# Reordering the first pass of a four-layer graph network kernel: where the aggregation, its casts and the transfers stand

## What is computed

```python
A_norm = A + eye(n);  deg = A_norm.sum(0) + A_norm.sum(1) - diagonal(A_norm);  dinv = rsqrt(deg)
agg = einsum('nm,bmd->bnd', A_norm * dinv[:, None] * dinv[None, :], x).reshape(-1, 256)
h   = relu(batchnorm(agg @ W1.T + b1))      # W1: 512 x 256, statistics over all 8192 rows
out = batchnorm(h @ W2.T + b2)              # W2: 256 x 512
```

## Time and profile before

| what | us |
|---|---|
| median of three runs (lowest, highest) | 2016.44 (2013.59, 2018.27) |
| time of the profiled execution | 2013.94 |
| its span in the trace | 2012.1 |
| TensorE busy | 1944.8 (97%) |
| TensorE weight loads busy | 1730.6 (86%) |
| VectorE busy | 1718.2 (85%) |
| ScalarE busy | 1443.6 (72%) |
| GpSimd busy | 187.8 (9%) |

### The profile page before, as it was taken

One profiled execution on the slowest core, in us unless ns is written; L12 is line 12 of the kernel. 1 busy time (PEld: TensorE's weight loads), 2 busy tenths in 40 slices (PEclk: granted clock), 3 DMA queues, 4 the chain that ended last, 5 costly groups with the idle time before them and its releaser, 6 DMA issues.

```text
span 2012.1 us, 85711 instructions
## 1 busy us (share of the span) xinstructions
PE 1944.8 (97%) x37031; PEld 1730.6 (86%) x37031; DVE 1718.2 (85%) x4795; ACT 1443.6 (72%) x4475; POOL 187.8 (9%) x258
## 2 busy tenths in 40 slices
PE   6899989999999999999999999999999999999997
PEld 3444469999999999999999999999999999999996
DVE  6779897888888988898889888898889888988866
ACT  5657537777777777767777777777777777777777
POOL 2000010110101010101001110101010101111000
PEclk9999999999999999999999999999999999999999
DMA  7857400000100001000100010000000010000000
GB/s 281 290 196 253 175 2 23 14 13 4 44 3 24 3 3 45 13 13 3 44 14 13 4 44 4 23 3 14 34 13 13 3 45 13 13 3 13 3 3 23
DMA packets 36822, 87.79 MB, mean 44 GB/s; under 512 B 2416, under 2 KB 26992, under 8 KB 32752
## 3 DMA queue, kind: packets, MB, share of 16 engines
q1 hardware_dynamic: 36464, 82.56, 11.8%
HBM read 52.15 MB, written 30.41 MB: 41 GB/s over the span
## 4 chain that ended last, share of the span: by engine, by line
PE 78%; ACT 5%; DVE 4%; issue 1%; POOL 0%; ACTq 0%; DVEq 0%
PE ps L1539 18%; PE ps L1568 11%; PE ps L1548 9%; PE ps L1353 8%; PE ps L1387 7%; PE ps L1575 5%; PE ps L1363 4%; PE ps L1395 3%; PE ps L468 2%; PE ps L1330 2%; ACT pool_mem L1726 2%; PE ps L1320 1%; PE ps L1627 1%; PE ps L1595 1%; PE ps L1441 1%; DVE stats L1849 1%
## 5 line engine op out<-in xcount | busy, mean ns | idle before, releaser
L1726 ACT ACTIVATE pool_mem<-ps,lstm_b 128x64 f32<-128x64 f32 (+2 forms) x2496 | 606.2, 364 | 147.0 <-PE ps L1575 102.6
L1539 PE MATMUL ps<-hl_a,w_hi 128*128 128x64 f16 (+1 forms) x3584 | 361.3, 205 | 1.8 <-DVE hl_a L2005 0.9
L1539 PE MATMUL ps<-hl_a,w_lo 128*128 128x64 f16 (+1 forms) x3584 | 360.8, 205 | 0.0
L1818 POOL TENSOR_TENSOR rstd<-mv,nhalf 128x2 f32<-128x2 f32 x224 | 174.1, 779 | 1592.3 <-DVE mv L1853 1592.3
L1539 PEld LDWEIGHTS ps<-hl_a,w_hi 128*128 128x128 f16 x3584 | 284.4, 97 | 6.3 <-DVE hl_a L2005 1.2
L1539 PEld LDWEIGHTS ps<-hl_a,w_lo 128*128 128x128 f16 x3584 | 283.0, 97 | 2.8
L1568 PE MATMUL ps<-pool_mem,w_hi 128*128 128x64 f16 (+2 forms) x3072 | 273.6, 200 | 0.0
L1568 PE MATMUL ps<-pool_mem,w_lo 128*128 128x64 f16 (+2 forms) x3072 | 273.5, 199 | 0.0
L1548 PE MATMUL ps<-hl_a,w_hi 128*128 128x64 f16 (+1 forms) x3584 | 233.5, 205 | 0.2 <-issue 0.2
L1568 PEld LDWEIGHTS ps<-pool_mem,w_hi 128*128 128x128 f16 x3072 | 228.9, 98 | 2.9
L1568 PEld LDWEIGHTS ps<-pool_mem,w_lo 128*128 128x128 f16 x3072 | 227.7, 98 | 0.7
(11 more groups left out here) (253 smaller groups left out, 4768.8 us busy)
## 6 DMA issues: line engine op xcount, KB each, us to landing
xa<-in_x SPq DMA_DIRECT2D x32, 512.0 KB, 5.4
h_scratch<-pool_mem SPq DMA_DIRECT2D x14, 1024.0 KB, 4.4
pool_mem<-h_scratch SPq DMA_DIRECT2D x14, 1024.0 KB, 6.8
pool_mem<-in_wpack SPq DMA_DIRECT2D x16, 704.0 KB, 4.2
out<-xb SPq DMA_DIRECT2D x16, 512.0 KB, 3.4
o_scratch<-act_in SPq DMA_DIRECT2D x14, 512.0 KB, 3.2
act_in<-o_scratch SPq DMA_DIRECT2D x14, 512.0 KB, 5.0
row<-in_rows SPq DMA_DIRECT2D x1, 1408.0 KB, 11.7
```

Source lines behind the costliest of these rows:

```text
L1539: nc.tensor.matmul(o, wk[part], toks[0][:, k], start=(g, m) == gms[0] and k == 0 and part == 0, stop=False, skip_group_check=True)
L1726: op = nc.scalar.activation(gates[s][h][:, g, m * w:(m + 1) * w], gate_place(s, h, g, m, w), ACT.Tanh, bias=lstm_b[:, bias:bias + 1], scal ...
L1818: nc.gpsimd.tensor_tensor(rstd[s][:, blocks(h)], mv[s][:, blocks(h), 1], nhalf[:, 0:HALF], ALU.pow)\
```

## The change

The work of the first pass is the same, instruction by instruction; its order on the engines changes.

1. TensorE: in the loop, `aggregate` of the other stream stands between the two halves of a stream's hidden layer, behind the first squaring: `hidden(0, first half)`, squaring, `aggregate(1, r+1)`, `hidden(0, second half)`, squaring, `hidden(1, first half)`, squaring, `aggregate(0, r+2)`, `hidden(1, second half)`, squaring. The first aggregation of stream 0 moves ahead of the loop; the last of stream 1 stands inside the last `hidden(0)`.
2. ScalarE: `hid_bias` takes a list of parts, and `agg_high` of the other stream and `unit_high` stand between its two halves.
3. VectorE: within a stream's part of a round: one `hid_stat`, squaring, one `hid_stat`, `agg_low` of the other stream, `unit_low`, squaring, two `hid_stat`.
4. SyncE: for each stream `store`, `load_unit`, `load_x`, in the place of two x loads followed by unit and store for each stream. The first x load stands ahead of the first two unit loads, the second behind them.
5. Opening: ScalarE casts stream 0's first aggregated tile before the first weight unit, VectorE does its low part before the first `unit_low`, and TensorE waits for that unit (`unit_lo`) before the loop. `SUMS` moves from bank 3 of stream 0 to bank 2 of stream 1.

```diff
-            GCN, SUMS = (ps[0][:, BANKS - 1, j * P:(j + 1) * P] for j in range(2))
+            GCN = ps[0][:, BANKS - 1, 0:P]
+            SUMS = ps[1][:, 2, 0:P]
...
+                load_x(0, 1, 2)
                 for b in range(STAGES):
                     load_unit(1, b)
-                with sp.Fori(1, ROUNDS - 1) as r:
+                load_x(1, 1, 2)
+                with sp.Fori(1, ROUNDS - 2) as r:
                     for s in range(STREAMS):
-                        load_x(s, r, r + 1)
-                    for s in range(STREAMS):
+                        store(s, r)
                         load_unit(r + 1, s)
-                        store(s, r)
-
+                        load_x(s, r + 1, r + 2)
                 for s in range(STREAMS):
+                    store(s, ROUNDS - 2)
+                    load_unit(ROUNDS - 1, s)
                     load_x(s, ROUNDS - 1, 0)
...
+                agg_high(0, 1)
                 unit_high(0, 0)
...
                 with act.Fori(0, ROUNDS - 1) as r:
-                    for s in range(STREAMS):
-                        agg_high(s, r + 1)
-                    for s in range(STREAMS):
-                        unit_high(r + 1, s)
-                        hid_bias(s, r + 1)
+                    hid_bias(0, r + 1, range(HT // 2))
+                    agg_high(1, r + 1)
+                    unit_high(r + 1, 0)
+                    hid_bias(0, r + 1, range(HT // 2, HT))
+                    hid_bias(1, r + 1, range(HT // 2))
+                    agg_high(0, r + 2)
+                    unit_high(r + 1, 1)
+                    hid_bias(1, r + 1, range(HT // 2, HT))
...
                 pe.wait_ge(step, 7)
+                aggregate(0, 1)
+                pe.wait_ge(unit_lo, 1)
                 with pe.Fori(0, ROUNDS - 1) as r:
-                    for s in range(STREAMS):
-                        aggregate(s, r + 1)
                     for s in range(STREAMS):
                         hidden(s, r + 1, range(HT // 2))
                         square(r * STREAMS + s, 0)
+                        aggregate(1 - s, r + 1 + s)
                         hidden(s, r + 1, range(HT // 2, HT))
                         square(r * STREAMS + s, 1)
-                for s in range(STREAMS):
-                    aggregate(s, ROUNDS)
-                hidden(0, ROUNDS, range(HT))
+                hidden(0, ROUNDS, range(HT // 2))
+                aggregate(1, ROUNDS)
+                hidden(0, ROUNDS, range(HT // 2, HT))
...
+                agg_low(0, 1)
                 unit_low(0, 0)
...
                 with dve.Fori(0, ROUNDS - 1) as r:
                     for s in range(STREAMS):
-                        agg_low(s, r + 1)
-                    for s in range(STREAMS):
+                        hid_stat(s, r, range(1))
+                        square(r * STREAMS + s, 0)
+                        hid_stat(s, r, range(1, HT // 2))
+                        agg_low(1 - s, r + 1 + s)
                         unit_low(r + 1, s)
-                        hid_stat(s, r, range(HT // 2))
-                        square(r * STREAMS + s, 0)
+                        square(r * STREAMS + s, 1)
                         hid_stat(s, r, range(HT // 2, HT))
-                        square(r * STREAMS + s, 1)
```

More of the change, by code:

```diff
@@ L680, in agg_high, with hid_bias @@
                     nc.scalar.copy(by_batch(hl_a[s][:, 0, :, :]), aggregated(s)).then_inc(agg_hi[s], 1)
[L682 to L685, removed]
+                def hid_bias(s, n, ms):
+                    if 0 in ms:
+                        act.wait_ge(hid_stored[s], n * 16 - 15)
+                        act.wait_ge(hid_stats[s], n)
+                    for m in ms:
                         act.wait_ge(hid_ps[s], n * HT - (HT - 1 - m))
@@ L699, in _ @@
                 with act.Fori(0, ROUNDS - 1) as r:
-                    for s in range(STREAMS):
-                        agg_high(s, r + 1)
-                    for s in range(STREAMS):
-                        unit_high(r + 1, s)
-                        hid_bias(s, r + 1)
-                for s in range(STREAMS):
-                    agg_high(s, ROUNDS)
-                for s in range(STREAMS):
-                    hid_bias(s, ROUNDS)
+                    hid_bias(0, r + 1, range(HT // 2))
[6 more added lines that the diff above has]
+                    hid_bias(1, r + 1, range(HT // 2, HT))
+                hid_bias(0, ROUNDS, range(HT // 2))
+                agg_high(1, ROUNDS)
+                hid_bias(0, ROUNDS, range(HT // 2, HT))
+                hid_bias(1, ROUNDS, range(HT))
             @block.tensor
@@ L781, in unit_low, with agg_low @@
                                                    ALU.subtract).then_inc(unit_lo, 1)
+                def agg_low(s, n):
+                    dve.wait_ge(agg_hi[s], n)
+                    nc.vector.tensor_tensor(by_batch(hl_a[s][:, 1, :, :]), aggregated(s), by_batch(hl_a[s][:, 0, :, :]), ALU.subtract)\
+                        .then_inc(agg_lo[s], 1)
                 dve.wait_ge(adj_in, 64)
@@ L828, in square @@
                             .then_inc(sq_ready, 1)
[L830 to L833, removed]
                 def hid_stat(s, r, ms):
@@ L859, in _ @@
                                                lam_part[:, 1:2]).then_inc(sq_ready, 1)
-                hid_stat(0, ROUNDS - 1, range(HT))
+                hid_stat(0, ROUNDS - 1, range(HT // 2))
+                agg_low(1, ROUNDS)
+                hid_stat(0, ROUNDS - 1, range(HT // 2, HT))
                 dve.wait_ge(hid_stats[0], ROUNDS + 1)
```

3 lines of the change are left out of this document (removed).

## The result

The changed kernel takes 2003.71 us (median of six runs, 2002.24 to 2006.43) against 2015.21 us (six runs, 2013.59 to 2018.27) for the kernel before: ratio 0.9944, 95% interval 0.9931 to 0.9957, 11.5 us or 0.56% faster. The forecast was 2004.4. The profiled execution took 2003.93 us, its span is 2002.1; before it was 2013.94 and 2012.1.

What follows compares the result with a forecast made beforehand. The first pass was taken as bound by TensorE plus one exposed chain per round. 10.36 (stalls) + 3.25 (opening) - 0.97 (aggregation) - 0.6 (edges) = 12.0 us off 2016.44 gave 2004.4, own range 2001 to 2007, 2000.5 to 2011 with rivals.

Steps and rivals of the forecast that it cites:

- Part 1: First-pass loop: rounds fall from 15.84 to 14.36 us without a wait, seven stalls of 1.48 us saved, 10.36 us.
- The edges: Loop: an aggregation alone rather than in a pair costs 0.04 us for each of 15, 0.6 us.
- Part 2: First-pass transfers: share rises to 0.92, each lands before its deadline, and the new order costs and gains nothing by itself.
- tight: Opening: second unit pair lands at about 21.8, wanted at about 22; a miss costs up to 1 us once.
- Part 3: Opening: TensorE starts hidden at 15.4 in place of 18.65, 3.25 us earlier, 2.28 net of one aggregation moved into the loop.
- cold spell: Opening: half-pace matmuls after TensorE's idle stretch cost 1.3 us; change taken as 0, possibly 1.6 more or 1.3 less.
- Part 4: End of first pass: 12.57 us becomes 13.54 with one aggregation inside; everything behind moves as a block, loads not late.
- Rival E: Stages behind the first pass fall otherwise on the clock: 2 us either way, counted in the range; no separate chance.
- Rival B: VectorE's queue makes agg_low late, TensorE waits twice a round; loses from VectorE 1.35 us later, 2025 us at worst; 4%.
- Rival A: Transfers become the bound of the first pass: share stuck at 0.85, rounds of 15.47 us, 2011.5 in total; chance 8%.

Runs made afterwards that it cites:

- late kernels: Changed kernel with one or two dummy bn_stats of 0.64 us each on VectorE ahead of agg_low inside the loop: 2006.11 and 2014.87 us.
- old transfers: Changed kernel with SyncE's first-pass order as before: both x loads, then unit and store for each stream; 2008.78 us.
- one bn_stats late: Changed kernel with one dummy bn_stats (0.64 us) on VectorE ahead of agg_low in the loop; 2006.11 us.
- half loads: Changed kernel with the second pass loading two of four parts of each hidden tile from its third tile on; 2002.06 us.
- warm with second order: Changed kernel with nine float32 matmuls filling TensorE's opening idle time, and second-pass loads and stores paired for each stream; 2000.17 us.

## Why the prediction was right

The mechanism was right: the stall is gone, and the chain has the slack that was worked out. That 2003.71 lies within 0.7 us of 2004.4 is in part luck, since the terms below, and what lies behind the first pass, came out up to 2 us to either side, and the same code gave 2001.81 and 2001.58 on other chips. One reading of the earlier trace rows was wrong: its digits are 7, 8, 5, 7 and 4, so the third slice is at 0.5, and the second pass loads the DMA engines as well.

- Part 1, the loop: right. Forecast 14.36 us a round without a wait, measured 14.29. The chain worked out from the rows of before (cast at 4.5 us from the half's start, low part 5.5 to 6.7, wanted at 7.18) is found at 4.35, 5.40 to 6.63 and 7.15. The slack of 0.5 us is 0.52 to 0.57 by the late kernels.
- The edges: too dear. I took 0.6 us; an aggregation next to a squaring costs (14.29 - 12.42) / 2 = 0.94 us, under the 0.97 of a pair's half. No edge is seen in the loop, so it saved 7 x 1.55 = 10.85 us.
- Part 2, the transfers: right for the new order, whose share is 0.90 to 0.94 by the window (forecast 0.92) with no wait; the unit that was "tight" in the opening brought none either. The words "costs and gains nothing by itself" were wrong as a view of the order: at this share the old order costs 7.0 us. I had compared each deadline with landings of before, and those had been measured at share 0.83. The Trainium skill's limit of about 358 GB/s ("DMA: Bandwidth & Descriptors", section Bandwidth) is no bound here: a round ran at 308 to 323 GB/s, but from 12 to 16 us the kernel before moved 427 GB/s and the kernel after 429, at a share of 1.05 in both. The same section says that 358 is each core's part when two cores stream, and that a core alone reached 425. So the 349 GB/s that the prediction worked out for share 1.0 isn't a ceiling either.
- Part 3, the opening: 3.58 us earlier against 3.25 forecast; 0.47 of it is that the first aggregation began at 8.85 and not 9.32. Of that, 0.17 is the transpose before it, which came earlier (7.41, not 7.58). The other 0.30 isn't scatter: from the transpose to the aggregation it is 1.43 to 1.44 us in all thirteen profiles that have the aggregation ahead of the loop, and 1.74 in the one of the kernel before; why is open. The cold spell lasted from 15.07 to about 19 and not 2.6 us. The half that it falls in took 9.11 us in place of 7.15, so it cost 1.96 us where I had 1.3, and where the kernel before paid 15.75 - 14.36 = 1.39 (its first round, without the wait at the end, against a later one): 0.6 us more, inside the 1.6 that I had left open. That the rise comes at another time in each execution of one code is seen too: the same half took 9.39 us in the second profile of the changed kernel and 8.56 in the third, and their passes ended at 131.11 and 130.32.
- Part 4 and the sum: the pass is 12.61 us shorter (forecast 12.0; the 19 matmuls at 130.85, forecast 131 to 132). By terms it is 10.85 + 3.58 - 0.94 - 0.57 (cold spell) = 12.92, and the last round gives back 0.3 of that: it takes 13.78 us from its start to the 19 matmuls, against 12.57 + 0.94. The profiled time fell only 10.0, since the second pass took 2.1 us more and what follows 0.5. That pass took 86.54 to 89.15 us in the eleven profiles in which its code is the same. Rival E put such scatter on the clock of the stages behind; that part is there as well, and is the larger one (1775.4 to 1779.0 us), but the second pass's I had not looked for. Medians say 11.5 on record, 12.9 and 13.6 us on the other chips.
- Rival B's mechanism and its point: the kernel with 1.28 us of delay lost all the gain in the total, where I had put the break-even at 1.35; by the end of its first pass, 2.1 us over 14 halves, it lies near 1.43. It wasn't at work in the changed kernel. Rival A wasn't either, but the old transfers show that it stood one edit away.
- The parts of the gain, from the runs: opening 2.0, loop with its transfers 10.8; and of that 10.8, 7.0 would be lost with the old order of transfers (4.8 of it seen in a trace). These parts don't add up one by one; the loop's 10.8 needs both.

## What to carry to other kernels

Where two streams share an engine, put one stream's head inside the other's body, and work out from the trace when the chain ends and when it is wanted; that half microsecond of slack was readable beforehand, and adding a known delay measures it. A shorter round raises the share of the transfers, so landing times of the slower kernel are too kind: issue each transfer when its buffer comes free, and test the old order too. In an in-order queue with two kinds of transfer, moving one kind forward can put the wait on the other, so look for the new wait before looking at the total.

## What I had not expected of the hardware

- TensorE's half pace came back in the middle of dense work: behind the sixteen matmuls of a single column at the end of the first pass (L773), in three of the fourteen executions profiled (one bn_stats late, half loads, and warm with second order). The row of 0.63 us follows a hidden layer that started at full pace; the granted clock of the window 128 to 130 us is 0.50, and from these sixteen matmuls to the 19 it takes 8.67 us in place of 6.98, 1.7 us more. It comes with some executions and not with others of the same code, and no run here tells why. In the half-loads kernel:
```profile
124.61 1.95 PE L773 MATMUL ps<-col,t 128*128 128x1 f32 x16
126.42 0.39 PE L454 MATMUL ps<-hl_a,w_hi 128*128 128x512 f16 x1
127.45 0.63 PE L454 MATMUL ps<-hl_a,w_hi 128*128 128x512 f16 x1
128.73 0.64 PE L454 MATMUL ps<-hl_a,w_hi 128*128 128x512 f16 x1
```
- One wait of 1.89 us in the old-transfers kernel was followed by a spell at half pace: the granted clock is 1.00 from 86 to 88 us, where the wait lies, and 0.59 and 0.55 in the next two stretches of 2 us.
- Executions of one kernel differ by 1.3 to 7 us, the second pass alone by 2.6 (86.54 to 89.15) and what follows it by 3.7 (1775.4 to 1779.0), so differences under 1.5 us between kernels are seen in the stages of a trace and not in the totals.
